# Score matmuls of two 32-row groups in one alternating call, the second pair behind the Q/gate projection

## What is computed

```python
xn = layernorm(x)
q, k, v = silu(xn @ Wq), silu(xn @ Wk), silu(xn @ Wv)      # 16 heads of 16
# in chunks, per head, with decay exp(ld):
scores  = (q_chunk @ k_chunk.T) * D                        # D: causal decay mask
o_intra = scores @ v_chunk
o_inter = (q_chunk @ S) * q_decay
S       = chunk_decay * S + (k_chunk * k_decay).T @ v_chunk
o = (o_intra + o_inter) * sigmoid((xn @ Wg1) @ Wg2)
o = o * rsqrt(mean(o * o, per head) + 1e-5) * norm_w
g = silu(fp8(xn * scale) / scale @ fp8(W2 * scale1) / scale1)
out = x + (o @ Wo) * g
```

## Time and profile before

| | |
|---|---|
| median of 3 runs | 194.22 us (193.96 to 195.49) |
| span of the profiled execution | 191.7 us, first to last instruction |
| median less span (launch and end) | 2.5 us |
| instructions | 6387 |
| PE / DVE / ACT / POOL busy | 90% / 83% / 54% / 55% |
| mean granted TensorE clock | 0.958 |
| L1082 score matmuls | 512 records, mean 283 ns |
| L717 masks | 64, mean 682 ns |

### The profile page before, as it was taken

One profiled execution on the slowest core, in us unless ns is written; L12 is line 12 of the kernel. 1 busy time (PEld: TensorE's weight loads), 2 busy tenths in 40 slices (PEclk: granted clock), 3 DMA queues, 4 the chain that ended last, 5 costly groups with the idle time before them and its releaser, 6 DMA issues.

```text
span 191.7 us, 6387 instructions
## 1 busy us (share of the span) xinstructions
PE 171.6 (90%) x1998; PEld 129.5 (68%) x1998; DVE 158.9 (83%) x548; ACT 103.2 (54%) x283; POOL 106.3 (55%) x181
## 2 busy tenths in 40 slices
PE   4867459999999999999999999999999999998392
PEld 4755238667776777777767777777767777776181
DVE  1869995889989898989897979898979798968672
ACT  3385336293848475665656473838383838372200
POOL 6954772555656465657574756565646556551210
PEclk9979966999999999999999999999999999999967
DMA  5383300000000010000000000000000000000000
GB/s 151 88 269 113 109 2 3 3 3 0 31 2 29 1 32 0 32 1 13 14 0 27 0 27 0 27 0 27 0 27 0 27 0 27 3 29 3 27 27 27
DMA packets 7199, 5.79 MB, mean 30 GB/s; under 512 B 1744, under 2 KB 7184, under 8 KB 7184
## 3 DMA queue, kind: packets, MB, share of 16 engines
q1 hardware_dynamic: 7184, 5.60, 9.3%
HBM read 3.50 MB, written 2.10 MB: 29 GB/s over the span
## 4 chain that ended last, share of the span: by engine, by line
PE 56%; DVE 20%; issue 12%; POOL 3%; DMA 3%; ACT 2%; DVEq 1%; SPq 1%; POOLq 0%; ACTq 0%
PE b_score L1082 9%; PE b_score L1121 9%; PE b_xo L1177 5%; PE b_att L1108 4%; DVE probs L717 4%; PE b_att L1140 3%; PE b_gate L1046 3%; PE b_xo L1169 3%; PE b_kv L1034 2%; PE b_kv L1031 2%; PE b_kv L1029 2%; PE b_qg L1029 2%; DVE shift L681 2%; PE b_att L1157 2%; DMA ld_row<-in_L_attn_log_decay_dram 2%
## 5 line engine op out<-in xcount | busy, mean ns | idle before, releaser
L717 DVE TENSOR_TENSOR probs<-b_score,decay_mask 128x512 f32<-128x512 f32 x64 | 43.5, 682 | 0.9 <-PE b_score L1082 0.5
L1082 PE MATMUL b_score<-qT,kT 32*64 32x128 f32 x512 | 31.6, 283 | 1.6 <-DVE probs L717 1.4
L545 ACT ACTIVATE xn<-x_sb,shift,rstd 128x256 f32 (+1 forms) x15 | 9.0, 602 | 42.3 <-DVE shift L681 42.3
L1082 PEld LDWEIGHTS b_score<-qT,kT 32*64 32x64 f32 x512 | 20.1, 132 | 12.3 <-issue 7.6
L374 POOL TENSOR_TENSOR state_c<-state,own_head 128x256 f32<-128x256 f32 x28 | 20.5, 734 | 11.6 <-DVE state L734 10.5
L344 POOL TENSOR_TENSOR e_sum<-e_y,e_magic 128x256 f32<-128x256 f32 x16 | 11.6, 727 | 20.5 <-DVE e_magic L692 20.5
L1121 PE MATMUL b_score<-probs,v_parity 128*32 128x128 f32 x512 | 17.9, 283 | 1.4 <-DVE probs L717 1.2
L383 POOL TENSOR_TENSOR on<-og,og_rs 128x256 f32<-128x256 f32 x15 | 9.3, 621 | 17.2 <-DVE og_rs L777 15.4
L1121 PEld LDWEIGHTS b_score<-probs,v_parity 128*32 128x32 f32 x512 | 13.6, 113 | 4.9 <-DVE probs L717 4.5
L775 DVE SCALAR_TENSOR_TENSOR og_half<-og_y,og_var 128x16 f32<-128x16 f32 x48 | 14.8, 309 | 0.7
L391 POOL TENSOR_TENSOR y<-sg,x_sb 128x256 f32<-128x256 f32 x15 | 10.9, 730 | 5.9 <-DVE sg L788 5.9
(11 more groups left out here) (136 smaller groups left out, 470.9 us busy)
## 6 DMA issues: line engine op xcount, KB each, us to landing
out_dram<-y SPq DMA_DIRECT2D x16, 128.0 KB, 1.7
x_sb<-in_L_attn_x_dram SPq DMA_DIRECT2D x3, 512.0 KB, 3.4
x_sb<-in_L_attn_x_dram SPq DMA_DIRECT2D x1, 384.0 KB, 4.6
w_f<-in_L_attn_Wk_dram SPq DMA_DIRECT2D x1, 256.0 KB, 2.8
w_f<-in_L_attn_Wv_dram SPq DMA_DIRECT2D x1, 256.0 KB, 3.0
w_f<-in_L_attn_Wq_dram SPq DMA_DIRECT2D x1, 256.0 KB, 3.0
w_f<-in_L_ffn_input_dram SPq DMA_DIRECT2D x1, 256.0 KB, 4.0
wo_f<-in_L_attn_Wo_dram SPq DMA_DIRECT2D x1, 256.0 KB, 3.8
```

What stands on the lines that cost most here:

```text
L717: v.tensor_tensor(probs[:, r].rearrange("p i (b c) -> p i b c", b=2), b_score[r % 2][:, 0:4 * C].rearrange("p (i c) -> p i c", i=4).unsque ...
L1082: mm = t.matmul(b_score[r % 2][c * C:c * C + C, half * 2 * C:(half + 1) * 2 * C], kT[rows, u, half, c * C:c * C + C], qT[rows, u, half, :, ...
```

## The change

`scores` takes a pair of groups instead of one group. Pair 0 is groups 0 and 1, pair 1 is groups 2 and 3; inside a call the matmuls go half by half, row half by row half, and for each of these first the even group into bank 0 and then the odd group into bank 1. Each group's last matmul still raises `s_score`. The wait ahead of pair 1 is for the masks 0 and 1 together. In the step the call for pair 0 takes the place of groups 0 and 1. The call for group 2 between the K/V and the Q/gate projection is gone; the call for pair 1 stands where group 3 stood, behind the Q/gate projection and behind `state_waits(i, j, 1)`. Number, shape and operands of the matmuls stay the same, and so do all other engines' programs.

```diff
-            def scores(i, j, r):
+            def scores(i, j, pair):
                 u = j % 2
-                if r == 0:
+                if pair == 0:
                     pe.wait_ge(s_qkT, 3 * (num(i, j) + 1))
                     need(pe, s_av, num(i, j))
-                need(pe, s_probs, 4 * num(i, j) + r - 1)
-                rows = slice(32 * r, 32 * r + 32)
+                need(pe, s_probs, 4 * num(i, j) + 2 * pair)
                 for half in range(KH):
                     for c in range(2):
-                        mm = t.matmul(b_score[r % 2][c * C:c * C + C, half * 2 * C:(half + 1) * 2 * C],
-                                      kT[rows, u, half, c * C:c * C + C], qT[rows, u, half, :, c * C:c * C + C],
-                                      start=True, stop=True)
-                mm.then_inc(s_score, 1)
+                        for lane in range(2):
+                            r = 2 * pair + lane
+                            rows = slice(32 * r, 32 * r + 32)
+                            mm = t.matmul(b_score[lane][c * C:c * C + C, half * 2 * C:(half + 1) * 2 * C],
+                                          kT[rows, u, half, c * C:c * C + C], qT[rows, u, half, :, c * C:c * C + C],
+                                          start=True, stop=True)
+                            if (half, c) == (KH - 1, 1):
+                                mm.then_inc(s_score, 1)
...
                 if cur:
                     scores(i, j, 0)
-                    scores(i, j, 1)
...
                 if nxt:
                     project_kv(i, j + 1)
-                if cur:
-                    scores(i, j, 2)
                 if first:
                     transpose_xq(0, 0)
...
                 if cur:
                     state_waits(i, j, 1)
-                    scores(i, j, 3)
+                    scores(i, j, 1)
                     state_step(i, j, 1)
```

## The result

The changed kernel takes 206.66 us (median of 4 runs, 205.88 to 207.29) against 194.17 us of the kernel before, run with it: a ratio of 1.0627 with a 95% interval of 1.0576 to 1.0678. Its profiled span is 204.7 us, 13.0 us longer. The forecast was slower, by 7.4 us, with a range that ended at 204.0. The sign and the place were right; the size was not.

What follows compares the result with a forecast made beforehand. It took each chunk as DVE's leg, then PE's. Mask 3's lateness, about 0.58 us in most chunks, less PE's own lateness in chunks 4, 8, 12 and 14, added 7.4 us: 201.6 us, range 198.0 to 204.0.

Steps and rivals of the forecast that it cites:

- What bounds the kernel (two legs): Each chunk: DVE's leg from mask 0 to mask 3's end, 6.23 us, then PE's to the next mask 0, 3.68 us.
- Part 1: First pair of score groups: they already run side by side, so alternating them by matmul costs 0.
- Part 2: PE sheds 0.68 us per chunk in chunks 1 to 14, inside DVE's leg; worth 0.6 us all told.
- Part 3, mask 2 late by 0.74: Chunk 6: the second pair waits for DVE's state addition, so mask 2 starts at 89.13 instead of 88.39.
- mask 3 0.58 us late: Chunk 6: og_y held by POOL's y, og_half by kd, so mask 3 starts at 90.41 instead of 89.83.
- The clock: Rival: added PE idle time ahead of the pair and from_chunk lowers the TensorE clock, adding beyond 202.8 us; 2%.
- Chunks 0, 14 and the end: Chunk 0 covered by PE's late from_chunk: 0; chunk 14 loses about 0.3 us; chunk 15, without a projection: 0.
- D: Rival: alternating groups no longer run side by side, a pair takes some 0.4 us more; 207 us, 3%.
- C: Rival: two small DVE steps keep their 1.44 us behind mask 2, mask 3 late by 0.74; 202.8 us, 8%.
- what was to show it: Signs in the profile after: about 0.7 us DVE idle before mask 2, pair 0.05 after state, chunks of 10.4 to 10.5.

Runs made afterwards that it cites:

- The move alone: Kernel before with groups 2 and 3, called one after the other, behind the Q/gate projection and the state wait: 203.39 us, ratio 1.0461.
- The filled kernel: Changed kernel plus three thrown-away identity matmuls on PE ahead of the wait for the state: 207.73 us, ratio 1.068 to the kernel before.
- the one with POOL's y and kd late: Changed kernel with POOL's y and kd moved behind head_norm: 204.4 us, ratio 1.0517 to the kernel before.
- The alternation alone: Kernel before with groups 0 and 1 alternating by matmul, groups 2 and 3 single and where they were: 194.42 us, ratio 1.0003.

## Why the prediction was wrong in size

**What bounds the kernel (two legs): right.** Shedding PE's block without a delay changes nothing (ratio 0.9969), from_chunk stays 0.05 us behind mask 3 in the kernel after, and the second leg kept its 3.67 us. **Part 1, alternation at 0: right** (1.0003). **Part 2: right**, 0.6 us at most; 194.35 against 195.1 has an interval that holds no change, and chunks 4, 8, 12 and 14 of that trace are 0.7 us shorter together.

**Part 3, mask 2 late by 0.74: mis-sized.** The hand-over from DVE's state addition to PE was taken as 0.05 us, the one seen at from_chunk; it is 0.13 (93.40 to 93.53). The 0.70 us from the pair to mask 2 were 0.71. So 0.83 in chunk 6. In chunks 3, 7 and 11, without that wait, 0.21 to 0.27 instead of 0.35: in chunk 7 the pair starts 0.85 us after the Q/gate projection (102.80 to 103.65) instead of 0.95.

**Part 3, "mask 3 0.58 us late, whichever time mask 2 has between 0.2 and 1.0 us late": the step that failed.** It holds in chunks 3, 7 and 11 (0.58), where og_y is issued 0.6 us ahead of kd. It also holds in 9 and 13 (0.61), where og_y is issued 10 ns behind kd and yet gets through. I had og_y issued 0.10 us ahead of kd, so that og_half would be the one held. With the hand-over 0.08 longer og_y came within 10 ns of kd's start, and in chunks 2, 5, 6 and 10, and in 4, 8 and 12, kd won: og_y is held for the whole of kd, og_half follows free, and mask 3 is 0.86 late. The exclusion was right, which of two POOL instructions catches which step was not. The cost: 0.3 us more in each of the seven, 2.1 us, less 0.2 in chunk 1, where POOL had no y to do. The move alone shows both outcomes a step apart: 20 ns earlier, and seven chunks lose 0.27 us less.

**The clock, put at nothing in the sum and at 2% among the rivals: the second step that failed.** Its 2.7 us are the largest part that is missing; without them the time would be 204.0, the end of the range. I had the idle time ahead of the pair right (0.5, measured 0.55) and half of that ahead of from_chunk (0.5, measured 1.00). I priced the chance from one row at clock 1.00, a row of a PE with nothing to wait for: it said nothing of a PE that is busy 9.23 of 10.78 us. What the two stretches cost is measured; why they come is not known. The filled kernel had none, but neither had the one with POOL's y and kd late, where PE idles as much.

**Chunks 0, 14 and the end, put at 0, 0.32 and 0:** 0.26, 0.49 and about 0.5 us. They were not taken apart by an experiment. The alternation alone, whose time is that of the kernel before, shows as much in chunk 0 (0.6) and at the end (0.9), so these 0.8 us may be no more than how two executions differ.

So 7.4 + 1.9 (og_y) + 2.7 (clock) + 0.9 (both ends and chunk 14) = 12.9 of 13.0 us. Of the rivals, D has the number (207) by luck: its mechanism, groups that no longer run side by side, did not happen (sixteen records in 0.67 us, ratio 1.0003). C (202.8) had the mechanism: the steps kept 1.46 us behind mask 2 in seven chunks, because og_y was held for the whole of kd. Of what was to show it, the idle time ahead of mask 2 (0.8 at most, in 15 chunks) and the 0.05 from mask 3 to from_chunk were there. og_half ending with kd and periods of 10.4 to 10.5 held only in part, and the pair came 0.13 behind the state instead of 0.05. That chunk 1 has no y on POOL, so that its mask 3 is late by 0.32 and not 0.58, could have been read from the trace before.

## What to carry over

Before work is moved behind a wait, ask what the engine that answers the wait does next: here the state addition stood directly ahead of the mask that needed the scores, so two engines that had overlapped took turns. Matmul time shed inside a leg that another engine sets is worth nothing by itself, and 6.6 us (together with the later state_step) once that leg is short, so the same edit must be judged again after each of its neighbours. Where small steps of DVE run between instructions of POOL, a delay does not pass through as it is: the next large step leaves when the POOL instruction ends that holds the last small one, and 10 ns can decide which step is held. A range has to hold both outcomes. And compare the clock of two traces chunk by chunk before a difference is put down to an edit: here two stretches at the low clock were as long as the whole gain of 2.3 us from the move on POOL.

## What the runs showed of the hardware

- A 128 x 16 step of DVE (0.17 us) issued within 10 ns of a POOL instruction's start is either through in 0.17 or held for 0.66 us. Both occur in one run (held in chunk 6, through in chunk 9, each issued 10 ns behind it).
- DVE's 128 x 256 steps with one SBUF input (e_exp, e_magic: 0.29 and 0.32 us on average) took 0.76 and 0.63 beside POOL.
- A PE that was busy 9.2 of 10.8 us per chunk lost its full clock in two of fourteen chunks, 1.4 us each. It kept it in two other kernels, busy 9.8 of 10.7 us in one and 9.2 of 11.0 in the other.
- Score matmuls of two row groups called one group after the other take 0.68 us for sixteen records (0.77 for some of the second pairs of the move alone), and alternating by matmul 0.67, where eight of one group take 0.65: side by side in both orders.
